# Third norm of a decoder layer: from TensorE transposes to two transposing transfers into two buffers

## The reference

```python
x = x + attn(layernorm(x))             # 16 heads, softmax over the rows, Toeplitz mixing of values
x = x + xattn(layernorm(x), ctx, ctx)  # causal cross attention to a context of 512 x 256
x = x + ffn(layernorm(x))              # 2 shared experts of 128, 16 routed of 64, top 2
def ffn(flat):
    out = einsum('tnm,nmd->td', silu(flat @ wg_s) * (flat @ wu_s), wd_s)
    probs = softmax(flat @ router_w); weights, indices = top_k(probs, 2)
    comb = one_hot(indices) * weights / sum(weights), summed over the 2 choices
    return out + sum over experts of (silu(flat @ wg_r) * (flat @ wu_r) * comb) @ wd_r
```

## Time and profile before

| quantity | value |
|---|---|
| median of 3 runs | 573.8 us |
| lowest, highest | 572.46, 576.2 us |
| profiled execution, its own time | 573.51 us |
| its span, first to last instruction | 571.7 us |
| PE busy | 541.9 us (95%) |
| DVE, ACT, POOL busy | 426.5, 255.7, 191.8 us |
| granted TensorE clock | 1.000 over the span |

### The profile page before, as it was taken

One profiled execution on the slowest core, in us unless ns is written; L12 is line 12 of the kernel. 1 busy time (PEld: TensorE's weight loads), 2 busy tenths in 40 slices (PEclk: granted clock), 3 DMA queues, 4 the chain that ended last, 5 costly groups with the idle time before them and its releaser, 6 DMA issues. The chain is left out here.

```text
span 571.7 us, 12923 instructions
## 1 busy us (share of the span) xinstructions
PE 541.9 (95%) x4716; PEld 368.2 (64%) x4716; DVE 426.5 (75%) x1107; ACT 255.7 (45%) x517; POOL 191.8 (34%) x240
## 2 busy tenths in 40 slices
PE   5787889999999999999999999999999998999997
PEld 4565557566685667766786668666866675666455
DVE  5858687868885787868886888778876776677654
ACT  4565546445354254445344445434543334332332
POOL 4215150223542144223522343234421343133123
PEclk9999999999999999999999999999999999999999
DMA  8995595795439903694449743993189125300351
GB/s 256 308 367 194 182 386 180 155 322 183 112 82 251 335 17 101 148 292 151 111 100 249 242 110 77 204 310 98 51 177 325 57 74 126 64 1 1 86 102 37
DMA packets 90734, 94.70 MB, mean 166 GB/s; under 512 B 28224, under 2 KB 76224, under 8 KB 90432
## 3 DMA queue, kind: packets, MB, share of 16 engines
q1 hardware_dynamic: 90688, 94.09, 58.1%
HBM read 75.66 MB, written 12.12 MB: 154 GB/s over the span
## 5 line engine op out<-in xcount | busy, mean ns | idle before, releaser
L694 POOL TENSOR_TENSOR mid<-gated,mid 128x512 f16<-128x512 f32 x72 | 86.6, 1202 | 214.0 <-ACT mid L880 213.9
L880 ACT ACTIVATE mid<-gated 128x512 f16<-128x512 f32 x72 | 44.9, 624 | 83.3 <-DVEq L1225 80.0
L146 PE MATMUL wide<-w_d,mid 128*128 128x256 f16 x288 | 78.5, 273 | 0.0
L148 PE MATMUL wide<-w_d,mid 128*128 128x256 f16 x288 | 78.5, 273 | 0.0
L147 PE MATMUL wide<-w_d,mid 128*128 128x256 f16 x288 | 78.5, 272 | 0.0
L1203 DVE SCALAR_TENSOR_TENSOR gated<-gated,score 128x512 f32<-128x512 f32 x72 | 49.1, 682 | 37.6 <-ACT gated L875 37.5
L146 PE MATMUL rows<-h3T,w_gu 128*128 128x512 f16 x160 | 60.7, 379 | 0.3 <-DVEq L126 0.3
L146 PE MATMUL score<-h3T,w_gu 128*128 128x512 f16 x160 | 60.7, 379 | 0.2
L147 PE MATMUL rows<-h3T,w_gu 128*128 128x512 f16 x160 | 60.6, 379 | 0.0
L148 PE MATMUL rows<-h3T,w_gu 128*128 128x512 f16 x160 | 60.6, 379 | 0.0
L148 PE MATMUL score<-h3T,w_gu 128*128 128x512 f16 x160 | 60.6, 379 | 0.0
(11 more groups left out here) (249 smaller groups left out, 1402.8 us busy)
## 6 DMA issues: line engine op xcount, KB each, us to landing
toep<-z_scratch SPq DMA_DIRECT2D x14, 2048.0 KB, 18.3
stage<-comb_scratch SPq DMA_DIRECT2D x32, 512.0 KB, 8.5
toep<-z_scratch SPq DMA_DIRECT2D x4, 1024.0 KB, 11.2
x_bo<-in_x SPq DMA_DIRECT2D x8, 512.0 KB, 11.8
x_in<-in_xr SPq DMA_DIRECT2D x7, 512.0 KB, 11.1
qT<-q_scratch SPq DMA_DIRECT2D x7, 512.0 KB, 3.9
vx<-v_scratch SPq DMA_DIRECT2D x7, 512.0 KB, 5.2
out<-x_out SPq DMA_DIRECT2D x7, 512.0 KB, 3.0
```

The costliest lines, as they stand in the source:

```text
L146: pe.matmul(out, stationary[0], moving[0], start=start, stop=False, **kw)
L148: return pe.matmul(out, stationary[1], moving[0], start=False, stop=stop, **kw)
L694: pool.tensor_tensor(mid_slot(j, 1, late), gate_slot(j, late), mid_slot(j, 0, late), ALU.subtract).then_inc(mid_split.sem, 1)
L880: act.activation(mid_slot(j, 0, late), gate_slot(j, late), ACT.Copy).then_inc(mid_hi.sem, 1)
```

## The change

In iterations 2 to 7 (`h3_moved`) h3 is no longer turned on PE. ACT copies each half of the rows to fp16 (`part_h3`, into the buffer of h2, free by then), POOL subtracts to make the low half, and SP issues two transposing transfers, one for all high parts and one for all low parts, 256 KB each. The destination alternates: h3T in odd iterations, the buffer cT in even ones. PE's logits wait for both transfers. ACT's first write to h2 in the next iteration (`take_rest`, q = 0) waits for them too. On SP `move_h1` now stands ahead of `fetch_context`, and `move_h3` behind it. The hardware loop of iterations 4 to 6 is written out on all engines. Iterations 1 and 8 turn h3 on PE as before.

```diff
@@ iterations, and the same in the PE block
-            with eng.Fori(2 + len(CONTEXT_IN), B - 1) as it:
+            for it in range(2 + len(CONTEXT_IN), B - 1):
                 iteration(it, True, True, True, True)
@@ new
+        def h3_moved(it):
+            return 2 <= it < B
+        def h3T_of(it):
+            return h3T if it % 2 else cT
+        def h3_rows(a):
+            return h2[:].rearrange("p c e -> p (c e)").bitcast(F16).rearrange("p (a k c e) -> p a c k e", a=2, k=K2, c=C)[
+                :, a]
@@ SP
+            def move_h3(it, b):
+                if it == 2:
+                    sp.wait_ge(ctx_taken.sem, ctx_taken.at(6, UNITS))
+                sp.wait_ge(rows.ready.sem, rows.is_ready(it - 1, f"u{MID - 1}"))
+                parts_of = h2[:].rearrange("p c e -> p (c e)").bitcast(F16).rearrange("p (a n) -> p a n", a=2)
+                for a, made in enumerate((h3_hi, h3_split)):
+                    hold(sp, made, made.at(b, 2))
+                    sp.dma_start(h3T_of(it)[:, a].rearrange("p k (c s) -> p (k c) s", s=P), parts_of[:, a],
+                                 transpose=True).then_inc(h3T_moved.sem, 16)
@@ SP iteration
+                if n and d:
+                    move_h1(it + 1)
                 if f and m:
                     fetch_context(it, it)
-                if n and d:
-                    move_h1(it + 1)
+                if h3_moved(it):
+                    move_h3(it, it - 1)
@@ POOL
+            def part_h3(b, half):
+                pool.wait_ge(h3_hi.sem, h3_hi.at(b, half + 1))
+                some = slice(2 * half, 2 * half + 2)
+                pool.tensor_tensor(h3_rows(1)[:, some], h3[:, some].rearrange("p c (k e) -> p c k e", k=K2),
+                                   h3_rows(0)[:, some], ALU.subtract).then_inc(h3_split.sem, 1)
...
                 for j in range(MID):
+                    if h3_moved(it) and j in (MID - 3, MID - 2):
+                        part_h3(it - 1, j - (MID - 3))
                     if d and j:
                         part_mid(it - 2, j)
@@ ACT
+            def part_h3(b, half):
+                act.wait_ge(h_ready[2].sem, h_ready[2].at(b, half + 1))
+                some = slice(2 * half, 2 * half + 2)
+                act.activation(h3_rows(0)[:, some], h3[:, some].rearrange("p c (k e) -> p c k e", k=K2),
+                               ACT.Copy).then_inc(h3_hi.sem, 1)
@@ ACT take_rest, q == 0
+                    if h3_moved(it - 1):
+                        act.wait_ge(h3T_moved.sem, h3T_moved.at(it - 2, 32))
@@ ACT iteration
                 for j in range(AHEAD, MID):
+                    if h3_moved(it) and j == MID - 2:
+                        part_h3(it - 1, 0)
                     if d and j < MID - 1:
                         part_mid(it - 2, j - 1)
                     if d:
                         tanh(it, it - 2, j)
+                    if h3_moved(it) and j == MID - 2:
+                        part_h3(it - 1, 1)
...
-                if d and m:
-                    act.wait_ge(rows.ready.sem, rows.is_ready(it, f"u{MID - 1}"))
-                if m:
-                    part_turned(it, it - 1, h3T, h3T_hi, "h3")
+                if m and not h3_moved(it):
+                    part_turned(it, 0 if it == 1 else 1, h3T_of(it), h3T_hi, "h3")
@@ DVE normalise
-                if n and not half:
+                if n == 2 and not half and h3_moved(it - 1):
+                    dve.wait_ge(h3_split.sem, h3_split.at(b, 0))
+                elif n and not half:
                     dve.wait_ge(turned.ready.sem, turned.was_ready(it, f"h{n + 1}.1"))
@@ PE logits (gate_up reads h3T_of(it - 1) too)
-                pe.wait_ge(turned.taken.sem, turned.is_taken(it - 1, "h3.1"))
+                if h3_moved(it - 1):
+                    pe.wait_ge(h3T_moved.sem, h3T_moved.at(it - 2, 32))
+                else:
+                    pe.wait_ge(turned.taken.sem, turned.is_taken(it - 1, "h3.1"))
@@ PE iteration
                     if d and m and j == MID - 1:
                         gate_up(it, j, some=slice(0, 1))
-                        turn_halves(it, "h3", h3, h_ready[2], it - 1)
+                        if not h3_moved(it):
+                            turn_halves(it, "h3", h3, h_ready[2], it - 1)
                         gate_up(it, j, some=slice(1, 2))
```

More of the change, by code:

```diff
@@ L371, in decoder_layer @@
         h3T_hi = sig("h3T_hi", 2)
+        h3_hi = sig("h3_hi", 2, -2)
+        h3_split = sig("h3_split", 2, -2)
+        h3T_moved = sig("h3T_moved", 32, -32)
         z_moved = sig("z_moved", 1, -2)
@@ L1611, in logits @@
                         last = three_passes(pe, rows.bank("logit")[:, NE * q:NE * q + NE],
-                                            parts(h3T, k, slice(P * q, P * q + P)), parts(w_r, k, slice(None)),
+                                            parts(h3T_of(it - 1), k, slice(P * q, P * q + P)), parts(w_r, k, slice(None)),
                                             start=(k == 0), stop=(k == K2 - 1))
@@ L1705, in gate_up @@
                                             parts(w_gu, k, slice(2 * P * j + at, 2 * P * j + at + P)),
-                                            parts(h3T, k, slice(None)), start=(k == 0), stop=(k == K2 - 1))
+                                            parts(h3T_of(it - 1), k, slice(None)), start=(k == 0), stop=(k == K2 - 1))
                     last.then_inc(banks.ready.sem, 1)
@@ L1901, in _ @@
                 iteration(it, True, True, True, True, c)
-            with pe.Fori(2 + len(CONTEXT_IN), B - 1) as it:
+            for it in range(2 + len(CONTEXT_IN), B - 1):
                 iteration(it, True, True, True, True)
```

## The result

The changed kernel takes 576.19 us in the median of 20 runs (574.34 to 578.38), the kernel before 573.73 us in 20 runs beside it: ratio 1.0037, 95% interval 1.0024 to 1.0050. It is slower by 0.4%, where I had forecast 568.4 us, 0.9% faster. The profiled execution has a span of 574.0 us against 571.7.

The account below looks back on a forecast made before the run. PE's own instructions were taken as the bound. Five turns at 0.87 us plus 1.0 us in iteration 7 gave 5.35 us off 573.51, so 568.2, and with 0.3 for the median 568.4 us; range 566.6 to 575.

Parts of the forecast that it names:

- The 0.87 us per turn: PE's eight transposes of h3 per turn cost 0.87 us from start to next start, removed in iterations 2 to 7.
- SP and the transfers: SP issues h1 in 2.65 us, is free by 336.4 (338.1 at worst), before the high half is ready at 338.5.
- High half 1: the second norm half ends at 337.60: Iteration 5: VectorE's second norm half ends at 337.60, so ACT's copy of the second high half ends at about 338.5.
- the deadline of 344.46: Iteration 5: PE reaches the logits at 344.46 without the turn; the low transfer was due at 343.7 to 344.1.
- a bad neighbourhood: GpSimd's low halves, priced as L694: 1.16 us each, or 1.50 as the worse bound.
- the slack of 0.2 us: Before `down` of block 9, slack shrinks from 0.4 to about 0.2 us; cost nothing, at worst 0.2 us each.
- The loop written out ... nothing either way: Iterations 4 to 6: equal windows (60.48, 60.50, 60.60 us) mean no gain or cost, bounds +-0.1 us each.
- landing 3.2 us later: Low transfer, issued at 340.5 to 340.9, lands 3.2 us later as the mix does; bounds 3.2 and 6.5 us.
- B: Rival: transfer lands later than the turn cost, PE waits 1.25 us at the logits; 576 us, 586 at the bound; chance 0.12.
- A: Rival: transfers queue behind the fetch, PE waits 0.4 to 0.8 us at the logits; about 571.5 us; chance 0.22.
- D: Rival: the turn was hidden, its removal exposing an equal wait such as `down` of block 9; 573.5 us; chance 0.05.
- C: Rival: PE's remaining gaps or the loop's jump shrink too, a further 0.3 us per iteration; 566.5 us; chance 0.07.

Follow-up runs that it names:

- e10: e9 with GpSimd also waiting for VectorE's first half of the second norm (h2) before block 1's low half: 570.54 us, ratio 0.9943 to the kernel before.
- e2: The kernel before with only `move_h1` issued ahead of `fetch_context`, loop kept: 573.63 us, ratio 0.9998.
- e1: The kernel before with only its hardware loop written out: 575.18 us against 573.68, ratio 1.0023.
- e3: The changed kernel, with GpSimd waiting for VectorE's second norm half before block 7's low half and making both h3 low halves behind that: 573.53 us, ratio 1.0001 to before.
- e4: The changed kernel with both h3 low halves made on VectorE, none on GpSimd: 572.92 us, ratio 0.9986 to the kernel before.
- e5: The changed kernel with the first h3 low half on GpSimd behind the second norm half, the second on VectorE: 574.66 us, ratio 1.0011 to before.
- e7: e4 plus an unneeded GpSimd subtraction of 128x512 where the changed kernel's first h3 subtraction stood: 583.39 us, ratio 1.0171 to the kernel before.
- e9: e4 with VectorE also making the low half of block 9 of the middle activations: 571.56 us, ratio 0.9959 to the kernel before.

## Why the prediction was wrong

**The 0.87 us per turn** were nearly right. The transposes' own share of iteration 5 is 0.84 us less after the change. In e10 the windows of iterations 4 to 6 are 0.65, 0.71 and 0.73 us shorter than before, since 0.1 to 0.2 us are still waited before the last `down`, and iterations 3 to 7 together 4.36 us.

**SP and the transfers** were right: h1's issue without a backlog 1.72 us (I took 2.65), SP free long before the high half, low landing 3.1 us after issue where no code packet met it (3.2), the order worth nothing (e2).

**The step that failed first** is "High half 1: the second norm half ends at 337.60". In the clock of the earlier trace rows it ended at 340.93 - 1.64 = 339.29. I had priced GpSimd's new subtraction in GpSimd's own time and asked only who waits for its data. I had not asked what VectorE does in those 1.16 us. With that 1.7 us, and 1.59 instead of 1.16 us for the operation itself, the second low half ended at 341.6 instead of 340.4 to 340.8 and landed at 344.8 instead of 343.7 to 344.1, 0.3 us behind the deadline of 344.46; and the gates of blocks 8 and 9 ran late, so that the slack of 0.2 us that I left to the last `down` turned into a wait of 0.27. Those two waits and 0.13 us before `down` of block 8 took 0.65 of the 0.87 us. The clue was in the earlier trace rows: the same L694 took 1.50 us once and 1.16 elsewhere. I called it "a bad neighbourhood" and made it a bound on GpSimd; it is a meeting of the two engines, seen from GpSimd's side. In the kernel before, seven of GpSimd's 128x512 operations began while VectorE's `gated<-gated,stage` (L1209, two inputs in SBUF) ran, and these took 1.4 to 1.5 us; of the other 96 all but one took 1.2 to 1.3.

The Trainium skill, SBUF — State Buffer, section "Who interferes with whom", says that GpSimd and VectorE share a pair of ports, that VectorE takes it in its two-port modes (a `tensor_scalar` can) or with two SBUF inputs against a GpSimd read, and that whoever comes first holds it for the whole instruction. Norm half against subtraction (2.46, 2.58 us) and subtraction against subtraction (1.64 us) agree with it; that the thing held is a port is the page's word, the runs show only that the operations exclude each other. With it an estimate could have been made from the earlier trace rows: two GpSimd operations in a row, 1.16 us each, are 2.3 us where the norm half has 0.74, so some 1.6 us per iteration. The norm half lost 1.72 us.

**The second step** is "The loop written out ... nothing either way". The windows I compared could not show it. Alone it costs 0.23% (e1). Worse, the sum had no term for code fetches in "landing 3.2 us later": in the changed kernel they met the low transfer in iterations 2 and 6, and it landed in 4.60 and 4.56 us. Against the 0.25 us of the others these waits cost about 2.0 and 1.5 us, of which the late landings are 1.5 each. Only that of iteration 6 can come from writing out the loop, since iteration 2 was written out before too; its fetch is a cost of putting a transfer with a deadline there. In the kernel before a code fetch had no transfer near a deadline to delay.

**The ledger** of the profiled pair: six turns and iteration 7's old wait -5.7; long waits in 2 and 6 about +3.5; the rest of the waits in iterations 2 to 7, and iteration 8's (+0.6, mostly for the mix), about +4.0 by difference; the start +0.5. In sum +2.3 us. How much of the +4.0 is the held norm's is not shown one by one; freeing the norm gave 2.7 us in e3 and 3.3 us in e4.

**The rivals.** The outcome has B's price, 576 us, by luck: the context fetch was out of the way as I had it, and PE waited longer for the low transfer than the turn had cost only in iterations 2 and 6. In the others there is a little of A (0.26 us before the logits) and of D (0.27 us before the last `down`), by a cause that neither names. C did not come. My range ended at 575.0, under B's own price; it should have held B, and a term for the engines' meeting.

## What to carry to other kernels

An operation moved to an idle GpSimd is not free because GpSimd has time: look at what VectorE runs in the same microsecond, and if it is an SBUF-to-SBUF `tensor_scalar` (0.74 us became 2.46 here) or has two SBUF inputs (0.69 became 1.64), add the GpSimd time to VectorE's chain, or hold GpSimd back with a wait. When work is taken off the engine that bounds, what ran beside it loses its cover too: find the next deadline of each chain, and the one after that (logits, then the last `down`). Where a transfer has a deadline with less than a microsecond in hand, code fetches belong in the range: here they cost 1.0 to 1.7 us when they met it, apart from one of 0.7.

## What the runs showed of the hardware that I had not expected

- VectorE's two-operation norm half of 0.74 us lasted 2.46 and 2.58 us beside two GpSimd operations in a row: each of its two instructions (0.41 us alone) ended 0.15 us after one of GpSimd's.
- A single 16 KB code packet went with a landing of 4.4 to 4.6 us instead of 3.1 for a transfer of 256 KB (3.8 to 4.8 over all eight kernels), though nearly all of the data had moved long before. In five kernels (e4, e5, e7, e9, e10) such a packet began 2.5 to 2.6 us after the issue in iteration 6 and the landing stayed at 3.1, while in iteration 2 it began 2.7 to 2.8 us after and the landing took 4.7 to 4.8; what separates the two is not shown.
- The issue of a 512 KB transposing transfer took 1.7 to 2.1 us with nothing ahead of it and 4.4 us behind 1 MB of fetches.
- The granted clock at the start differs from run to run of one kernel (mean over the span 0.993 to 1.000 in the kernel before). In the changed kernel's profile it fell to the lower of its two levels after PE had idled for 1.95 us behind the first transposes.
